# Packed constants and initial states, three filler products, one epsilon moved, and a new step list in a Test-Time-Training layer

## The chip, the cores and the metric

The kernel runs on one core of a Trainium2 chip, as one hand-ordered program for all engines. The metric is the device time of one execution in microseconds (us), taken as the median of three runs. The profile is of one further execution.

## The reference

For each of 4 sequences of 512 tokens and 256 channels the layer computes, in float32:

```
x = x + layernorm(attn(layernorm(x)));   x = x + layernorm(ffn(layernorm(x)))
attn: qkv = x @ Wqkv; q, k = l2norm(silu(.)) per head of 64; v = silu(.)
      lr = softplus(x @ Wlr + c); mom = sigmoid(x @ Wm + bm); scale = silu(x @ Ws + bs)
      for each chunk of 128 tokens, states W0, W1, W2 (64x64 a head), momenta M0, M1, M2:
          out = (silu(q W0^T) * (q W2^T)) W1^T
          dW0, dW1, dW2 = gradients from k, v and lr, plus M * mean(mom);  M = dW
          dW = newton_schulz5(dW):  five times A = X X^T; B = bA + cA A; X = aX + B X
          W  = renorm(W + dW)
      out = rmsnorm(out) * g * scale, plus windowed softmax attention with 128-wide heads
      result @ Wo
ffn:  gelu(x @ proj1^T + b1) @ proj2^T + b2      (1024 hidden)
```

## The kernel before

All five engines walk the same list of steps, `ORDER`. A step is a kind, a chunk and an index (`NA.1.3.0` is kind NA, chunk 1, iteration 3, state 0). Each engine runs the parts of those kinds that it takes a share in and skips the others, so the list fixes the program order on every engine at once; between engines there are only semaphore waits. `bank_plan` derives the PSUM banks from the same list. SyncE (SP) alone doesn't follow the list before the change: its loads and stores stand in a fixed sequence.

The kinds that matter here, with the TensorE (PE) line that a profile shows:

- `LN1`/`LNX` the first layer norm, `XT` its transposes (L536 for chunk 0, L543 later), `QK` (L559) and `VV` (L568) the projections, `TR` (L591) transposes of q, k, v.
- `FW` (L629), `GB` (L604), `DH` (L617), `OUT` (L643), `DW` (L662) the chunk's forward and gradient products; `SS` (L673) the Frobenius norms.
- the Newton-Schulz steps, five iterations over three states in each of chunks 0 to 2: `TX` (L682, four 128x128 transposes), `NA` (L691), `NB` (L701), `NX` (L713). ScalarE (ACT) copies after TX and NX, VectorE (DVE) finishes NA and NB.
- `RN`/`RM` the renorm of the states, `WX` (L723) the transposes of the new states.
- `S`, `PT`, `PV`, `CT`, `WO` (L732, L739, L748, L755, L763) attention and output projection; `NT` (L770), `F1` (L782), `F2`/`F2N` (L793) the feed-forward block and its norm.

`NA`, `NB`, `NX`, `DH`, `FW` and `OUT` run on 64x64 quarters of the PE array, four at a time, `GB` on 64x128 halves, and the others on all 128 rows. `NA`, `NB` and `NX` leave 32 records a step (64x64x64 products), `F1` 4 of 512 columns, `TX` 4.

The start of chunk 0. PE first runs nine 128x128 products of ones (L808), then `XT.0.0`, then `QK.0.0`. SP issues x for sequence 0, all of Wqkv, x for the others, three small weight pieces, seven small constants (b1 in elements of 4 bytes), and, when Wqkv has landed, six pieces of the initial states into `w_in`. DVE's `WI` copies them into `W` in six copies (L1355, L1359), ACT's `WI` squares them (L1022), and `WX.0.0` to `WX.0.2` transpose `W` on PE, with three ACT copies. The first layer norm of a sequence is DVE statistics, then GpSimd (POOL) for variance plus epsilon (L1424) and the power -0.5 (L1419), then DVE.

SP's later sequence is: x again for chunks 0 and 1, x for chunks 2 and 3, the stores of chunk 0, x again for chunk 2, the stores of chunk 1, x again for chunk 3, and the rest of the stores. The loads of `x again` (L451) each wait for the one before to land.

The end, for the last sequence of the last chunk: `F2` on PE, then

```
dve.bn_stats(st4[:, b, :], f2[:, b, :])
dve.bn_aggr(mv4[:, b, :], st4[:, b, :])
pool.tensor_scalar(var[:, sl], mv[:, sl, 1], LN_EPS, None, ALU.add)   # L1424
tt(rstd[:, sl], var[:, sl], neg_half[:, 0:k], ALU.pow)                # L1419
```

then the scaling on DVE and the store.

Of the kernel before, what the change touches and what calls it, by code (L numbers as in the profile page):

```python
# [30 lines left out]
P = 128  # L31
# [3 lines left out]
HD = 64  # L35
# [5 lines left out]
SMALL = 5 * NH  # L41
LN_EPS = 1e-5
# [81 lines left out]
NOT_IN_FIRST = ("x_in", "ln1_stats", "ln1_mv", "ln1_var", "ln1_rstd", "xn", "xT_ps", "xnT", "mm_ps", "mm", "decayed")  # L124
# [4 lines left out]
def steps(text):  # L129
# [7 lines left out]
    LN1.0.0 XT.0.0 LNX.0.0 LN1.0.1 LN1.0.2 CO.0 LN1.0.3 LNX.0.1 QK.0.0 XT.0.1 LNX.0.2 LNX.0.3 VV.0.0 VV.0.1 SI.0.0  # L137
    NQ.0.0 XT.0.2 XT.0.3 QK.0.1 SI.0.1 WI.0 LN1.1 QK.0.2 VV.0.2 NQ.0.1 LNX.1 SI.0.2 NR.0.0 QK.0.3 VV.0.3 NR.0.1 NQ.0.2
    TR.0.0 SM.0 TR.0.1 SI.0.3 MS.0 NQ.0.3 TR.0.2 TR.0.3 XT.1 TR.0.4 TR.0.5 TR.0.6 TR.0.7 NR.0.2 NR.0.3 KL.0.0 KL.0.1
    KL.0.2 KL.0.3 SP.0 WX.0.0 WX.0.1 WX.0.2 S.0.0 S.0.1 VV.1.0 VV.1.1 TR.0.8 TR.0.9 WN.0 FW.0.0 FE.0.0 FE.0.1 DH.0  # L140
    FW.0.1 GB.0.0 GB.0.1 OUT.0.0 OUT.0.1 EL.0.0 EL.0.1 OE.0 QK.1.0 SI.1.0 QK.1.1 EY.0 SI.1.1 S.0.2 ELB.0.0 ELB.0.1
    PT.0.0 PT.0.1 MU.0.0 MU.0.1 MU.0.2 MR.0.0 MR.0.1 MR.0.2 QK.1.2 DW.0.0 DW.0.1 QK.1.3 SS.0.0 S.0.3 SS.0.1 OY.0
    VV.1.2 PV.0.0 PV.0.1 SS.0.2 PT.0.2 PT.0.3 SN.0.0 SN.0.1 VV.1.3 CT.0.0 PV.0.2 PV.0.3 SN.0.2 WO.0.0 TX.0.0.0
    TX.0.0.1 CT.0.1 NA.0.0.0 NA.0.0.1 SI.1.2 CT.0.2 WO.0.1 TX.0.0.2 NB.0.0.0 NB.0.0.1 CT.0.3 NA.0.0.2 NX.0.0.0
    NX.0.0.1 WON.0.0 WON.0.1 L2.0.0 NB.0.0.2 TX.0.1.0 WO.0.2 WO.0.3 NA.0.1.0 L2N.0.0 WON.0.2 WON.0.3 NX.0.0.2 SM.1
    L2.0.1 L2.0.2 TR.1.0 TX.0.1.1 TX.0.1.2 L2.0.3 TR.1.1 NA.0.1.1 NA.0.1.2 NB.0.1.0 L2N.0.1 L2N.0.2 L2N.0.3 TR.1.2
    TR.1.3 NB.0.1.1 NB.0.1.2 NT.0.0 MS.1 NT.0.1 NT.0.2 NT.0.3 NX.0.1.0 NX.0.1.1 NX.0.1.2 TX.0.2.0 NQ.1.0 TX.0.2.1
    TX.0.2.2 NQ.1.1 SI.1.3 F1.0.0 NA.0.2.0 NA.0.2.1 NA.0.2.2 F1.0.1 F1.0.2 LN1.2 NB.0.2.0 NB.0.2.1 NB.0.2.2 NQ.1.2
# [18 lines left out]
    F2.1.3 XT.3 GB.2.0 GB.2.1 EL.2.0 EL.2.1 OUT.2.0 OUT.2.1 S.2.1 ELB.2.0 ELB.2.1 OE.2 QK.3.0 QK.3.1 QK.3.2 MU.2.0
    MU.2.1 MU.2.2 DW.2.0 DW.2.1 PT.2.0 PT.2.1 QK.3.3 MR.2.0 MR.2.1 MR.2.2 SS.2.0 S.2.2 SS.2.1 SS.2.2 S.2.3 OY.2 SN.2.0
    PV.2.0 PV.2.1 SN.2.1 SN.2.2 PT.2.2 VV.3.0 PT.2.3 PV.2.2 CT.2.0 F2N.1.1 CT.2.1 TX.2.0.0 TX.2.0.1 TX.2.0.2 NA.2.0.0
    NA.2.0.1 SI.3.0 NA.2.0.2 WO.2.0 WO.2.1 NB.2.0.0 NB.2.0.1 NB.2.0.2 NX.2.0.0 NX.2.0.1 NX.2.0.2 WON.2.0 WON.2.1  # L170
    L2.2.0 TX.2.1.0 TX.2.1.1 TX.2.1.2 PV.2.3 NA.2.1.0 NA.2.1.1 NA.2.1.2 NQ.3.0 F2N.1.2 L2N.2.0 VV.3.1 VV.3.2 NB.2.1.0
# [1407 lines left out]
```

## Time and profile before

| | before |
|---|---|
| median of three runs | 382.04 us (381.73 to 382.21) |
| span of the profiled execution | 380.1 us |
| what lies around the span, to the median | 1.9 us |
| PE busy | 371.0 us, 98% |
| DVE, ACT, POOL busy | 68%, 56%, 51% |

In the rows below a line is a time, a duration, an engine, a source line and what it writes and reads, with the number of records. In the chain of waits the pieces follow each other in time without overlap, so the length of a piece is the time until the next piece; in the timeline the last product of a group includes its way through the array, so groups overlap by some 0.2 us.

### The profile page before, as it was taken

The page shows a single profiled execution, that of the slowest core. Times are in us where ns is not written, and L with a number is a line of the kernel's source. Part 1 is how long each engine was busy: PE and PEld are TensorE (multiplying, and loading weights), DVE is VectorE, ACT ScalarE, POOL GpSimd, SP SyncE. Part 2 cuts the span into 40 slices and gives each one's busy share as a digit, 9 for nine tenths or more (in the row PEclk, how much of TensorE's full clock was granted, in tenths as well). Part 3 has the DMA queues.
Part 4 walks back from the last instruction along what each step waited for, and adds up shares of the span by engine and source line. Part 5 has one row for each costly group of instructions (what it writes and reads, how often), then busy time and mean ns, then how long its engine had stood idle before and what let it go on. Part 6 is the DMA issues. An engine that isn't in the chain of part 4 may idle for free.

```text
span 380.1 us, 15979 instructions
## 1 busy us (share of the span) xinstructions
PE 371.0 (98%) x6760; PEld 295.4 (78%) x6760; DVE 257.6 (68%) x682; ACT 213.3 (56%) x432; POOL 193.9 (51%) x290
## 2 busy tenths in 40 slices
PE   8999999999999999999999999999999999999994
PEld 5588688856788877878578888688887757988883
DVE  4678998674278699898546746987875492767124
ACT  1799855766512766649743346665358575614500
POOL 4399865356239457475963434364333340557212
PEclk9999999999999999999999999999999999999999
DMA  5562200001000000000000200000000110000101
GB/s 156 121 238 60 83 1 6 3 3 46 16 3 2 3 3 2 3 4 5 16 19 17 71 16 3 2 2 17 20 3 4 40 36 2 0 3 0 57 0 55
DMA packets 12677, 10.84 MB, mean 29 GB/s; under 512 B 4544, under 2 KB 12096, under 8 KB 12608
## 3 DMA queue, kind: packets, MB, share of 16 engines
q1 hardware_dynamic: 12608, 9.83, 8.9%
q8 instruction: 54, 0.88, 1.0%
q14 instruction: 15, 0.12, 0.1%
HBM read 7.73 MB, written 2.10 MB: 26 GB/s over the span
## 4 chain that ended last, share of the span: by engine, by line
PE 86%; DVE 4%; SPq 3%; issue 2%; POOL 2%; ACT 1%; DMA 1%; POOLq 0%; DVEq 0%; ACTq 0%
PE pair L782 15%; PE pair L793 15%; PE pair L713 6%; PE pair L701 6%; PE pair L691 6%; PE pair L559 6%; PE pair L682 5%; PE pair L591 4%; PE pair L763 3%; PE pair L732 3%; PE pair L568 3%; PE pair L748 3%; PE pair L662 2%; PE pair L739 2%; PE pair L629 1%
## 5 line engine op out<-in xcount | busy, mean ns | idle before, releaser
L782 PE MATMUL pair<-xn2T,p1T 128*128 128x512 f32 (+1 forms) x160 | 59.1, 512 | 0.0
L793 PE MATMUL pair<-p2T,h 128*128 128x256 f32 x256 | 57.0, 379 | 0.0
L793 PEld LDWEIGHTS pair<-p2T,h 128*128 128x128 f32 x256 | 48.0, 190 | 6.4 <-issue 0.2
L1424 POOL TENSOR_SCALAR var<-mv 128x1 f32<-128x1 f32 (+1 forms) x55 | 13.1, 239 | 67.1 <-DVE mv L1382 37.4
L1034 ACT ACTIVATE h<-pair,b 128x512 f32<-128x512 f32 (+1 forms) x40 | 23.9, 602 | 36.0 <-PE pair L782 35.9
L782 PEld LDWEIGHTS pair<-xn2T,p1T 128*128 128x128 f32 x160 | 28.7, 190 | 17.1 <-issue 14.8
L1419 POOL TENSOR_TENSOR nq<-ssq,half 128x8 f32<-128x8 f32 (+1 forms) x16 | 24.2, 1513 | 27.5 <-DVE ssq L1141 27.5
L1056 DVE SCALAR_TENSOR_TENSOR A<-pair,eye 128x512 f32<-128x512 f32 x45 | 28.7, 683 | 13.2 <-PE pair L691 13.1
L1419 POOL TENSOR_TENSOR rstd<-var,neg_half 128x1 f32<-128x1 f32 (+1 forms) x55 | 33.5, 609 | 4.6
L1056 DVE SCALAR_TENSOR_TENSOR B<-pair,eye 128x512 f32<-128x512 f32 x45 | 28.9, 684 | 10.2 <-PE pair L701 10.0
L559 PE MATMUL pair<-wqkv,xnT 128*128 128x512 f32 x64 | 31.5, 627 | 0.6 <-ACT xnT L816 0.6
L701 PEld LDWEIGHTS pair<-A 64*64 64x64 f32 x1440 | 23.7, 134 | 7.5 <-issue 4.6
L987 ACT ACTIVATE masked<-masked,nmax 128x256 f32<-128x256 f32 (+1 forms) x32 | 15.1, 474 | 25.5 <-DVE nmax L1298 25.5
L823 ACT ACT_TABLE_LOAD x22 | 28.2, 1283 | 1.1 <-PEq L1569 0.7
L691 PEld LDWEIGHTS pair<-XT 64*64 64x64 f32 x1440 | 23.3, 134 | 6.3 <-issue 5.7
L816 ACT ACTIVATE XT<-pair 128x512 f32<-128x512 f32 x45 | 24.6, 600 | 6.4 <-PE pair L682 6.4
L713 PEld LDWEIGHTS pair<-X,B 64*64 64x64 f32 x1440 | 23.6, 134 | 5.0 <-issue 2.7
L959 ACT ACTIVATE X<-pair 128x512 f32<-128x512 f32 x36 | 19.8, 598 | 13.2 <-PE pair L713 13.1
L701 PE MATMUL pair<-A 64*64 64x64 f32 x1440 | 26.5, 221 | 0.3 <-issue 0.3
L713 PE MATMUL pair<-X,B 64*64 64x64 f32 x1440 | 26.1, 221 | 0.1
L691 PE MATMUL pair<-XT 64*64 64x64 f32 x1440 | 25.8, 221 | 0.3 <-ACT XT L816 0.2
L682 PE MATMUL pair<-ident,X 128*128 128x128 f32 x180 | 24.1, 276 | 0.5 <-ACT X L959 0.3
(165 smaller groups left out, 775.4 us busy)
## 6 DMA issues: line engine op xcount, KB each, us to landing
x_in<-in_L_attn_x_dram SPq DMA_DIRECT2D x16, 128.0 KB, 2.5
x<-in_L_attn_x_dram SPq DMA_DIRECT2D x16, 128.0 KB, 2.1
out_dram<-rows_a SPq DMA_DIRECT2D x16, 128.0 KB, 1.7
p1T<-in_L_ffn_proj_dram SPq DMA_DIRECT2D x1, 1024.0 KB, 4.7
p2T<-in_L_ffn_proj_dram SPq DMA_DIRECT2D x1, 1024.0 KB, 7.4
wqkv<-in_L_attn_Wqkv_dram SPq DMA_DIRECT2D x1, 768.0 KB, 4.8
wo<-in_L_attn_Wo_dram SPq DMA_DIRECT2D x1, 256.0 KB, 7.7
X<-in_L_attn_w_dram SPq DMA_DIRECT2D x6, 32.0 KB, 2.2
```

Source lines behind the costliest of these rows:

```text
L559: mm_ = pe.matmul(ps, xnT[:, k, b * P:(b + 1) * P], wqkv[:, k, 0:512], start=(k == 0), stop=(k == KC - 1))
L682: mm_ = pe.transpose(ps[:, b * P:(b + 1) * P], X[:, g, 2 * b:2 * b + 2, :], ident[:, :])
L691: mm_ = pe.matmul(BANK[bank[0] + row][64 * col:64 * col + 64, n * HD:(n + 1) * HD], xt, xt, start=True, stop=True)
L701: mm_ = pe.matmul(BANK[bank[0] + row][64 * col:64 * col + 64, n * HD:(n + 1) * HD], a, a, start=True, stop=True)
L713: mm_ = pe.matmul(BANK[bank[0] + row][64 * col:64 * col + 64, n * HD:(n + 1) * HD], B[64 * row:64 * row + 64, g, 4 * (row ^ (slot & 1)) + ...
L782: mm_ = pe.matmul(ps[:, at], p1T[:, k, n * P:(n + 1) * P], xn2T[:, k, at], start=(k == 0), stop=(k == KC - 1))
L793: mm_ = pe.matmul(ps[:, 0:DIM], h[:, n, b * P:(b + 1) * P], p2T[:, n, :], start=(n == 0), stop=(n == HC - 1))
L816: return act.activation(dst, src, ACT.Copy)
L823: act.preload_act_table_set(name)
L1034: act.activation(h[:, n, at], BANK[bank[0]][:, at], ACT.Gelu, bias=b1[:, n:n + 1]).then_inc(S["h"].sem, 1)
L1056: return dve.scalar_tensor_tensor(out=out_, in0=in0, scalar=scalar, in1=in1, op0=op0, op1=op1)
L1419: return pool.tensor_tensor(out_, in0, in1, op)
```

## The change

- **Loads.** The host lays out three arrays: `Wall` (Wqkv, Wlr, Wm, Ws side by side), `packed` (all constants as each lane holds them, 356 values a lane), and `states` (the initial W, as the kernel holds it for all sequences, and its transposes, 3072 values a lane). SP issues x of sequence 0, the 512 columns of q and k, x of the others, the 276 other columns, `packed`, W, and the transposes in two pieces, and no longer waits for Wqkv in between. Bytes that these loads move: 128, 512, 3 times 128, 276, 178, 768, 512 and 256 KB.
- **Work gone.** DVE's `WI` (six copies), one memset, `WX.0.0` to `WX.0.2` (12 PE transposes, three ACT copies). ACT's `WI` waits for the load of W.
- **Three products on ones.** After the transposes of `XT.0.0` PE runs three products of 128x128 on 64 columns into bank 7.
- **Last epsilon.** For the last sequence of the last chunk DVE adds epsilon, POOL only takes the power.
- **SP follows the list.** `XA` (x again), `XI` (x for a chunk) and the stores (`F2N`) are steps of the list. `XA` of chunk 2 or 3 waits for all four `outb` of two chunks before.
- **A new list.** The same steps otherwise, in another order; `EY` and `WN` move to the front, `KL.0.3` behind `EL.0.1`, and the Newton-Schulz steps of a state are no longer taken three by three.

```
-            sp.dma_start(wqkv[:, :, 0:3 * DIM], Wqkv...).then_inc(ld_qkv, 16)
+            sp.dma_start(wqkv[:, :, 0:512], Wall[:, 0:512]...).then_inc(ld_qkv, 16)
...
+            sp.dma_start(wqkv[:, :, 512:], Wall[:, 512:]...).then_inc(ld_v, 16)
+            sp.dma_start(packed_in[:, :], packed).then_inc(ld_misc, 16)
+            sp.dma_start(W[:, :, :, :], states[:, 0:1536]...).then_inc(ld_w, 16)
+            sp.dma_start(WT02[:, :, :, :, :], states[:, 1536:2560]...).then_inc(ld_wT, 16)
+            sp.dma_start(W1T[:, :, :, :], states[:, 2560:3072]...).then_inc(ld_wT, 16)
+            XI(1)
...
+            def XA(c):
+                if c >= 2:
+                    sp.wait_ge(*S["outb"](c - 2, BATCH))
+                for b in range(BATCH):
+                    if b or c:
+                        sp.wait_ge(*S["x_again"](c, 16 * b))
+                    sp.dma_start(x1[:, c % 2, b, :], ...).then_inc(S["x_again"].sem, 16)
...
                     mm_.then_inc(S["first_xT"].sem, 1)
+                    if b == 0:
+                        for n in range(3):
+                            pe.matmul(BANK[7][:, 0:64], ones[:, :], ones[:, 0:64], start=True, stop=True)
...
             def WI(c):
-                act.wait_ge(*S["W"](0, 3))
+                act.wait_ge(ld_w, 16)
...
             def F2(bank, c, b):            # DVE
+                if ends(c, b):
+                    dve.wait_ge(*S["f2_mv"](c, b + 1))
+                    dve.tensor_scalar(var4[:, b:b + 1], mv4[:, b, 1:2], LN_EPS, None, ALU.add)...
...
             def F2(c, b):                  # POOL
+                if ends(c, b):
+                    wait_apart(pool, S["f2_var"](c, b + 1))
+                    tt(rstd4[:, b:b + 1], var4[:, b:b + 1], neg_half[:, 0:1], ALU.pow)...
+                    return
```

The start of the list, and a stretch in chunk 1's Newton-Schulz steps:

```
-    LN1.0.0 XT.0.0 LNX.0.0 LN1.0.1 LN1.0.2 CO.0 LN1.0.3 LNX.0.1 QK.0.0 XT.0.1 LNX.0.2 LNX.0.3 VV.0.0 VV.0.1 SI.0.0
+    LN1.0.0 XA.0 XT.0.0 WI.0 LNX.0.0 QK.0.0 XT.0.1 CO.0 LN1.0.1 LN1.0.2 XT.0.2 LNX.0.1 SI.0.0 LN1.0.3 EY.0
+    LNX.0.2 LNX.0.3 WN.0 VV.0.0 NQ.0.0 XT.0.3 QK.0.1 VV.0.1 LN1.1 VV.0.2 SI.0.1 NQ.0.1 QK.0.2 SI.0.2 NR.0.0
...
-    NX.1.3.2 TX.1.4.0 TX.1.4.1 TR.2.4 TX.1.4.2 TR.2.5 TR.2.6 MP.2 KL.2.3 F2N.0.2 NA.1.4.0 NA.1.4.1 NA.1.4.2 TR.2.7
-    F1.1.6 NB.1.4.0 F2N.0.3 NB.1.4.1 NB.1.4.2 TR.2.8 F1.1.7 NX.1.4.0 NX.1.4.1 NX.1.4.2 RN.1.0 RN.1.1 RM.1.0 RN.1.2
+    TX.1.4.0 F1.1.5 NR.2.3 TX.1.4.1 F2N.0.3 NB.1.3.2 NA.1.4.0 MM.2 NA.1.4.1 NX.1.3.2 NB.1.4.0 KL.2.2 F1.1.6
+    TX.1.4.2 F1.1.7 NA.1.4.2 NB.1.4.1 TR.2.4 MP.2 NX.1.4.0 NB.1.4.2 RN.1.0 NX.1.4.1 F2.1.0 TR.2.5 RN.1.1 TR.2.6
```

In the new list `XA.2` stands in chunk 0's third Newton-Schulz iteration, ahead of all `F2N.0` steps. `F2N.0.3` stands 15 PE steps ahead of `F2.1.0`, whose DVE part waits until chunk 0's stores have landed.

## Rows read from the trace of the kernel before

**Rows 1.** The page: the span, and TensorE's share of it.

```profile
span 380.1 us, 15979 instructions
PE 371.0 (98%) x6760; PEld 295.4 (78%) x6760; DVE 257.6 (68%) x682; ACT 213.3 (56%) x432; POOL 193.9 (51%) x290
```

**Rows 2.** Windows, TensorE alone: busy time and, behind it, the granted clock.

```profile
54.00:120.00 66.00, 65.59 (x1653) 1.00 0.04 11
```

**Rows 3.** Timeline of TensorE, 0 to 30 us; in brackets the idle time before.

```profile
1.04 4.21 PE L808 MATMUL pair<-ones 128*128 128x128 f32 x18 [1.04 <-DVE ones L1054]
5.28 0.66 PE L536 MATMUL pair<-ident,rows_b 128*128 128x128 f32 x2
6.50 3.75 PE L559 MATMUL pair<-wqkv,xnT 128*128 128x512 f32 x4 [0.56 <-ACT xnT L816]
...
17.16 1.88 PE L559 MATMUL pair<-wqkv,xnT 128*128 128x512 f32 x4
```

**Rows 4.** Timeline of ScalarE, 0 to 50 us.

```profile
5.98 0.38 ACT L816 ACTIVATE xnT<-pair 128x256 f32<-128x256 f32 x1 [3.98 <-PE pair L536]
10.29 0.60 ACT L816 ACTIVATE raw<-pair 128x512 f32<-128x512 f32 x1 [3.94 <-PE pair L559]
...
16.24 1.01 ACT L1022 ACTIVATE B<-W 128x256 f32<-128x256 f32 x3
```

**Rows 5.** Chain of waits, chunk 0's second Newton-Schulz iteration.

```profile
77.36 1.56 PE pair L691 x96
78.92 3.63 PE pair L782 x8
82.55 1.56 PE pair L701 x96
84.11 3.63 PE pair L782 x8
87.74 1.56 PE pair L713 x96
89.30 1.48 PE pair L682 x12
90.78 1.72 PE pair L782 x4
92.50 1.56 PE pair L691 x96
```

**Rows 6.** Chain of waits, chunk 2's fourth and fifth iterations.

```profile
276.38 0.87 PE pair L682 x8
...
289.27 1.09 PE pair L701 x64
...
290.83 1.91 PE pair L782 x4
292.74 0.62 PE pair L701 x32
```

**Rows 7.** Chain of waits, the transposes of the initial states.

```profile
25.33 1.31 PE pair L723 x12
```

**Rows 8.** Timeline of SyncE's queue: loads of x again, stores.

```profile
181.41 28.27 SPq L491 DMA_DIRECT2D out_dram<-rows_a  x4
209.72 7.29 SPq L451 DMA_DIRECT2D x<-in_L_attn_x_dram  x4
```

**Rows 9.** Windows, TensorE alone, while the feed-forward weights land; last GB/s.

```profile
21.00:22.00 1.00, 1.00 (x11) 1.00 1.08 386
```

**Rows 10.** Chain of waits, from the last product's end.

```profile
361.14 13.83 PE pair L793 x64
374.97 0.02 issue
375.00 0.44 DVE rows_a L1378
...
376.33 0.22 POOL var L1424
376.55 0.04 issue
376.59 0.83 POOLq L236
```

More of the change, by code:

```diff
@@ L167 @@
[L167 to L171, printed above, removed]
@@ new lines @@
+    FE.1.1 QK.2.1 ELB.1.0 ELB.1.1 OUT.1.0 OE.1 MU.1.0 OUT.1.1 MU.1.1 DW.1.0 MU.1.2 MR.1.0 DW.1.1 PT.1.0 S.1.2
+    MR.1.1 QK.2.2 PT.1.1 S.1.3 SS.1.0 MR.1.2 QK.2.3 OY.1 SS.1.1 PV.1.0 SN.1.0 SS.1.2 PT.1.2 PV.1.1 CT.1.0 VV.2.0
+    TX.1.0.0 SN.1.1 VV.2.1 NA.1.0.0 CT.1.1 SN.1.2 TX.1.0.1 WO.1.0 SI.2.0 NB.1.0.0 NA.1.0.1 TX.1.0.2 F2N.0.0
+    PT.1.3 PV.1.2 NA.1.0.2 WON.1.0 NB.1.0.1 WO.1.1 PV.1.3 NX.1.0.0 NB.1.0.2 NX.1.0.1 CT.1.2 WON.1.1 L2.1.0
+    NQ.2.0 TX.1.1.0 SI.2.1 CT.1.3 VV.2.2 TX.1.1.1 SI.2.2 NA.1.1.0 WO.1.2 NA.1.1.1 NB.1.1.0 WON.1.2 NX.1.0.2
@@ new lines @@
+    RN.2.1 RM.2.0 RN.2.2 RM.2.1 RM.2.2 TR.3.5 F1.2.4 F1.2.5 WX.3.0 FE.3.0 F1.2.6 WX.3.1 WX.3.2 F1.2.7 FE.3.1
+    FW.3.0 FW.3.1 PT.3.0 PT.3.1 MS.3 OE.3 S.3.2 OUT.3.0 OUT.3.1 S.3.3 F2.2.0 F2.2.1 OY.3 PV.3.0 PT.3.2 F2.2.2
+    PV.3.1 PT.3.3 CT.3.0 F2N.2.0 PV.3.2 F2N.2.1 CT.3.1 WO.3.0 WO.3.1 WON.3.0 PV.3.3 WON.3.1 L2.3.0 CT.3.2 L2.3.1
+    L2N.3.0 L2N.3.1 F2.2.3 CT.3.3 NT.3.0 WO.3.2 NT.3.1 WO.3.3 WON.3.2 F1.3.0.0 F1.3.1.0 F1.3.2.0 F1.3.3.0
+    WON.3.3 F1.3.4.0 L2.3.2 F1.3.5.0 L2.3.3 F1.3.6.0 NT.3.2 L2N.3.2 NT.3.3 F1.3.7.0 F1.3.0.1 F1.3.1.1 F1.3.2.1
@@ L184 @@
+    L2N.3.3 F1.3.3.1 F2N.2.2 F2N.2.3 F1.3.4.1 F2.3.0 F1.3.5.1 F1.3.6.1 F1.3.7.1 F2N.3.0 F2.3.1 F2.3.2 F2N.3.1
+    F2N.3.2 F2.3.3 F2N.3.3
 """)
@@ L231, with layer_kernel @@
 PLAN = bank_plan(ORDER)
-def layer_kernel(nc, x, Wqkv, Wlr, Wm, bm, Ws, bs, Wo, w0, w1, w2, o_norm_g, qk_scale, qk_offset,
-                 proj1T, proj1_bias, proj2T, proj2_bias, out):
+def layer_kernel(nc, x, Wall, packed, states, Wo, proj1T, proj2T, out):
     with ExitStack() as ctx:
@@ L434, in mask_of, with ends @@
             return mask[:, seen(c):2 * P] if slot(c) else mask[:, P:3 * P]
+        def ends(c, b):
+            return c == CHUNKS - 1 and b == BATCH - 1
         def learns(c):
@@ L459, in rows_in, with F2N @@
                     sp.dma_start(x_in[:, b, :], x[b, bass.ts(c, CHUNK), :]).then_inc(S["x_in"].sem, 16)
+            def F2N(c, b):
+                sp.wait_ge(*S["outb"](c, b + 1))
+                sp.dma_start(out[b, bass.ts(c, CHUNK), :], outb[:, b, :]).then_inc(S["stored"].sem, 16)
+            parts = {"XI": XI, "XA": XA, "F2N": F2N}
             sp.dma_start(x_in[:, 0, :], x[0, 0:CHUNK, :]).then_inc(first_x[0], 16)
-            sp.dma_start(wqkv[:, :, 0:3 * DIM], Wqkv.rearrange("(k p) n -> p k n", p=P)).then_inc(ld_qkv, 16)
+            sp.dma_start(wqkv[:, :, 0:512], Wall[:, 0:512].rearrange("(k p) n -> p k n", p=P)).then_inc(ld_qkv, 16)
@@ L485, in _, with run @@
             sp.dma_start(wo[:, :, :], Wo.rearrange("(k p) n -> p k n", p=P)).then_inc(ld_wo, 16)
-            rows_again(0)
-            def stores(c):
-                for b in range(BATCH):
-                    sp.wait_ge(*S["outb"](c, b + 1))
-                    sp.dma_start(out[b, bass.ts(c, CHUNK), :], outb[:, b, :]).then_inc(S["stored"].sem, 16)
-            rows_again(1)
-            rows_in(2)
-            rows_in(3)
-            stores(0)
-            rows_again(2)
-            stores(1)
-            rows_again(3)
-            stores(2)
-            stores(3)
+            def run(order):
+                for kind, c, *arg in order:
+                    if kind in parts:
+                        parts[kind](c, *arg)
+            run(ORDER)
             sp.wait_ge(*S["stored"](CHUNKS, 0))
```

172 lines of the change are left out of this document (81 added, 91 removed).

## The prediction

 So PE's order of work is the critical path, and other engines count only where they make PE wait. PE's idle time is 9.1 us: 1.04 before the first product and 0.56 before the first QK [rows 3], 5.1 from the last product's end at 374.97 to the end [rows 10], and 2.4 spread over everything else. The reader is to see that there is little idle time to win, and that what PE spends on a piece of work is what counts.
>
> Busy does not mean at peak, though. I walked through PE's steps from XT.0.0 at 5.28 to 374.97, which is 369.7 us, and gave each step the shortest time that a step of its kind with such neighbours has anywhere in this trace. That adds up to 357 us, so 12 us are waits or slow stretches: 1.8 in QK.0.0, 1.0 just before it, and about 9 in small pieces, most of them under 0.5 us. These 9 us are an estimate, and all that a better order can give back.
>
> **The work that goes.** The transposes of the initial states are 12 records, 1.31 us of PE in the chain [rows 7]: **-1.3**. DVE's copies and ACT's copies go too; both engines are far from full [rows 1], so that alone is worth nothing.
>
> **What the new list costs on PE.** This is the term that decides. In the chain a block of 64x64 products takes 0.62 us for one step, 1.09 for two, 1.56 for three [rows 5, 6]: 0.47 a step, and 0.15 once a block. Blocks on all 128 rows pay too when they stand between such blocks: F1 with 4 records takes 1.72 where it ends a run begun by TX, 1.91 alone between 64-row blocks, and two of them 3.63, not 3.44; TX with 12 records takes 1.48, where 8 take 0.87, so 12 would take 1.31 [rows 5, 6]. So each 128-row run pays 0.15 to 0.19, and each time PE goes over to 64-row products and back costs 0.30 to 0.34 us. The stretch from 77.36 to 92.50 checks it: 15.14 us, of which 9 Newton-Schulz steps at 0.47, five F1 at 1.72 and 1.31 of transposes are 14.14; three returns cost the other 1.0 [rows 5].
>
> I counted in both lists how many separate runs of 64-row steps (NA, NB, NX, DH, GB, FW, OUT) PE meets: 52 before, 70 after. The new list mixes states and iterations singly with transposes and other work, where the old one took three at a time. 18 more at 0.32: **+5.8** (5.4 to 6.1). No cover hides it, since PE itself is the bound.
>
> The Trainium skill, page TensorEngine Tiling (Array Packing), section Key Properties, says that changing the tiling mode drains TensorE; by its wording every change of mode counts, also those to DW's 128x64 tiles and GB's 64x128, of which I count 114 before and 147 after. It gives no price; with half of the 0.32 for each of 33 more the term would be +5.3, not +5.8. It speaks against this change as the rows do.
>
> **The start.** Nine products on ones take 4.21 us as 18 records, and QK.0.0 3.75 us, where a later QK takes 1.88; the transposes of XT.0.0 are slow as well [rows 3]. That is the 1.2 GHz level, though the windows show no lower granted clock there. PE was at work from 1.04 on, with one gap of 0.56 us before QK.0.0. Three products of 64 columns fit in that gap: at this rate some 0.1 a record, six records, 0.6 us. PE's wait is for ACT's copy, which ends at 6.36 [rows 4], so they delay nothing. If the full rate comes by 7, QK.0.0 gains up to 1.8 us; if it comes as late as before, nothing. The trace has no such case, so these are the bounds.
>
> Not all of it can be kept. ACT's WI now stands ahead of the copies of QK.0.0 and XT.0.1, and waits for W. Up to W's end the queue moves 2.2 MB (the sizes in the section on the change); at the 386 GB/s of [rows 9] this is 5.8 us, from about 2 or 3 us on, so W lands at 8 to 9. The squares take 1.0 [rows 4], then the copy of q and k 0.6 and of xnT 0.4 must follow before QK.0.1: about 11. PE at full rate is done with QK.0.0, two XT, VV.0.0 and XT.0.3 at about 10, and stands still for 1 us. At the old rate ACT is free at 6.36 to 10.29 [rows 4], which covers WI, and nothing is lost or won. I take half: **-0.9** (0 to -1.8).
>
> The Trainium skill, page TensorE: Matmul & The Clock Gate, Part 1, says that throttled is the default state and sustained activity releases it, whatever the number of products. By that rule the filled gap would bring the full rate earlier, and the term could be the whole -1.8.
>
> **Other waits.** EY and WN leave POOL's busy stretch for its idle beginning, the initial states need no preparation, and Newton-Schulz steps of different states follow each other in a pipeline. I compared, for every producer and consumer on PE, how much PE work lies between them in both lists: in both nearly all distances are about the shortest that the trace shows to suffice (1.0 us for NA to NB and NB to NX). So the new list is no worse, and may avoid some of the 9 us. Half of these pieces are under 0.1 us and stay in any order. I take **-2.0**, with bounds of -5 (all but these gone) and +1.5.
>
> **SP's queue.** XA.2 stands ahead of chunk 0's stores and waits for all four outb. When F2N.0.3 is done, four loads must go first, 7.3 us for three of the intervals and so some 9.5 with the last [rows 8], then four stores at about 0.5, and a landing of 2: some 12 us after outb. F2.1.0's part on DVE needs them, 15 PE steps and its own 3.5 us later, by my prices 13.6 us after F2N.0.3. outb itself costs 1 to 2 us. It just fits: 0, and if it does not, DVE stands still, and with it the renorm of chunk 1. The transposed states have landed long before FW.0.0, the first to read them, which follows all of chunk 0's projections.
>
> **The end.** After the last product come DVE, POOL's epsilon (0.22 us, with 0.15 before it), POOL's power and DVE [rows 10]. On DVE the epsilon saves one step to another engine but takes its own time: **-0.1** (0 to -0.2). The subtraction behind it still ends ahead of POOL's power of 0.83.
>
> **Sum.** -1.3 + 5.8 - 0.9 - 2.0 - 0.1 = +1.5 on a span of 380.1: 381.6. Around the span lie 1.9 us to the median of the runs, 382.04. So 383.5.
>
> **Rivals.** First, the other side: the new order takes nearly all waits away, and the full rate comes early. -1.3 + 5.8 - 1.8 - 5.0 - 0.1 = -2.4: 379.6. For it speaks the finer pipeline and POOL's lighter middle; against it, that PE has only 2.4 us of true idle time there [rows 1]. It decides from the point where start and waits together give back more than 5.2 us. Chance 0.25. Second, the three products release nothing and the order saves no waits: -1.3 + 5.8 - 0.1 = +4.4: 386.4. For it: 4.2 us of products and XT did not release the clock before [rows 3]. Chance 0.12. Third, the stores of chunk 0 land too late: if the loads take 2.4 us each and outb comes 2 us after F2N.0.3, DVE waits 1 to 2 us at F2.1.0: 385.0. Chance 0.08. The forecast has 0.55.
>
> **Numbers.** 0.2% is 0.76 us, about what a measurement of this kernel can tell from no change. The forecast's own spread is 381 to 385.5; of its 0.55 some 0.15 lies within 0.76 us of 382.04 and 0.03 below. With the first rival that makes faster 0.28, within 0.2% 0.16, slower 0.56. The range runs from 380.0 to 386.0: it leaves out about half of the first and second rivals.
>
> **What would show it.** In the changed profile the Newton-Schulz lines L691, L701, L713 should appear in the chain as many blocks of 32 and 64 records at 0.62 and 1.09, and F1 or transposes between them with 0.15 to 0.19 extra; PE busy should be about as long as now or longer, though 12 transposes are gone. QK.0.0 should take 1.9 to 3.75 us and be followed by a wait for ACT behind the squares. The chunk 0 stores come after four loads, and DVE should not wait for them. The prediction is wrong if the extra returns are cheaper than 0.3 us where both sides are single steps, or if the waits that remain are under 4 us in all.

## The result, and the profile after

The changed kernel takes 386.77 us (median of four, 385.51 to 387.03), the kernel before beside it 382.12: ratio 1.0112, with a 95% interval of 1.0095 to 1.0129. So slower, as forecast, but by 4.7 us and not by 1.5, and above the range's 386.0.

The page of the changed kernel, to be read against [rows 1]:

```profile
span 385.1 us, 15941 instructions
...
PE 375.3 (97%) x6754; PEld 296.7 (77%) x6754; DVE 259.2 (67%) x676; ACT 213.6 (55%) x429; POOL 194.3 (50%) x289
...
PEclk9899999999999999999999999999999999999999
...
q8 instruction: 54, 0.88, 1.0%
```

PE is busy 4.3 us longer with six records fewer, and still 3.1 us longer in a second profile in which the clock does not fall: the order costs more than the transposes gave back. The second of its 40 slices, 9.6 to 19.3 us, has a lower granted clock, which no slice of before has. Why is in the timeline of TensorE:

```profile
6.85 1.94 PE L553 MATMUL pair<-wqkv,xnT 128*128 128x512 f32 x4
...
12.69 2.92 PE L553 MATMUL pair<-wqkv,xnT 128*128 128x512 f32 x4 [2.23 <-ACT xnT L810]
```

and in that of ScalarE:

```profile
10.76 1.03 ACT L1017 ACTIVATE B<-W 128x256 f32<-128x256 f32 x3 [4.35 <-DMA W<-in_states_dram]
11.70 0.57 ACT L810 ACTIVATE raw<-pair 128x512 f32<-128x512 f32 x1
12.18 0.65 ACT L810 ACTIVATE xnT<-pair 128x256 f32<-128x256 f32 x2
```

QK.0.0 runs in 1.94 us (3.75 in [rows 3]). Meanwhile ACT stands 4.35 us for W, which lands at 10.7, and the copies for QK.0.1 come behind the squares. W was issued at 4.14 us; the page has the 6.6 us to its landing:

```profile
W<-in_states_dram SPq DMA_DIRECT2D x1, 768.0 KB, 6.6
```

```profile
13.50:17.00 3.50, 3.50 (x7) 1.90 (x6) 0.69 (x1) 2.26 (x5) 2.92 (x2) 0.51 0.31 79
```

The middle looks as the forecast said. The chain of waits in chunk 0's third iteration, against [rows 5]:

```profile
85.03 1.72 PE pair L776 x4
86.75 0.62 PE pair L695 x32
87.38 0.47 PE pair L685 x32
87.84 1.91 PE pair L776 x4
89.76 0.44 PE pair L676 x4
90.19 0.44 PE pair L585 x4
90.63 0.62 PE pair L695 x32
```

Blocks of one or two 64-row steps stand where three stood; the first costs 0.62, one behind it 0.47, and F1 alone between them 1.91. But further on the chain has a thing that the forecast didn't know:

```profile
303.46 0.62 PE pair L707 x32
304.09 0.23 PE pair L695 x16
304.32 0.67 issue
304.99 0.40 PE pair L695 x10
```

PE stops for 0.67 us in the middle of one NB step, where no instruction waits for a semaphore.

SP's queue did as forecast: four loads of 6.5 us, then the stores of chunk 0, all issued by 214.5, three us ahead of DVE's part of F2.1.0, which waits for PE and for no transfer:

```profile
204.84 6.54 SPq L456 DMA_DIRECT2D x<-in_L_attn_x_dram  x4
211.42 3.07 SPq L468 DMA_DIRECT2D out_dram<-rows_a  x4
...
217.50 0.42 DVE L1359 TENSOR_TENSOR rows_a<-pair,packed_in 128x256 f32<-128x256 f32 x1 [1.77 <-PE pair L787]
```

The tail's chain has DVE's epsilon, 0.16 us for POOL's 0.22 and its 0.15 ahead of it [rows 10]. POOL's power behind it takes 0.59 us in the chain, where it took 0.83 behind POOL's own epsilon. From the last product to the end are 4.8 us instead of 5.2:

```profile
381.48 0.16 DVE var L1366
```

**The account.** I walked through all PE steps of the changed kernel as the prediction did for before, each at the cheapest price that its kind and neighbours have in the trace of before. The first three rows are this count and no view of the profile; it ends PE's work 0.1 to 0.2 us ahead of the chain's last product, which the fifth row takes up. A second profile of the same program (e11 below) is beside it. A fetch is the load of a stretch of PE's own instructions; the experiments on the stops show why it stands here.

| us | before | changed | changed, again |
|---|---|---|---|
| PE's steps at the cheapest price | 357.4 | 362.4 | 362.4 |
| above it, up to TX.0.0.0 | 5.3 | 7.5 | 5.6 |
| above it, behind TX.0.0.0 | 6.8 | 4.8 | 6.2 |
| of these, stops of over 0.15 inside 64x64 blocks at a fetch | 0.5 | 1.9 | 3.1 |
| ahead of the first transpose, and the tail | 10.6 | 10.4 | 10.4 |
| span | 380.1 | 385.1 | 384.6 |

### The profile page after: what moved, and what is told of

Its sections match the earlier page's. It is cut to its first block, busy times and chain, and to the rows that moved or that the text cites. A ratio compares the mean times of both kernels' runs of the same rounds, so it can differ in the third digit from the quotient of the medians.

```text
span 385.1 us, 15941 instructions
## 1 busy us (share of the span) xinstructions
PE 375.3 (97%) x6754; PEld 296.7 (77%) x6754; DVE 259.2 (67%) x676; ACT 213.6 (55%) x429; POOL 194.3 (50%) x289
## 4 chain that ended last, share of the span: by engine, by line
PE 95%; ACT 0%; DVE 0%; issue 0%; POOLq 0%; DVEq 0%; ACTq 0%
PE pair L776 15%; PE pair L787 15%; PE pair L553 7%; PE pair L695 7%; PE pair L685 6%; PE pair L707 6%; PE pair L676 6%; PE pair L585 5%; PE pair L562 4%; PE pair L757 4%; PE pair L726 3%; PE pair L742 3%; PE pair L656 2%; PE pair L623 2%; PE pair L733 2%; PE pair L598 2%
## 5 line engine op out<-in xcount | busy, mean ns | idle before, releaser
L1051 DVE SCALAR_TENSOR_TENSOR B<-pair,eye 128x512 f32<-128x512 f32 x45 | 30.5, 684 | 18.3 <-PE pair L695 18.0
L1029 ACT ACTIVATE h<-pair,packed_in 128x512 f32<-128x512 f32 (+1 forms) x40 | 24.1, 602 | 33.1 <-PE pair L776 32.9
L1051 DVE SCALAR_TENSOR_TENSOR A<-pair,eye 128x512 f32<-128x512 f32 x45 | 30.5, 687 | 14.9 <-PE pair L685 14.5
L810 ACT ACTIVATE XT<-pair 128x512 f32<-128x512 f32 x45 | 26.5, 594 | 15.4 <-PE pair L676 15.2
L685 PE MATMUL pair<-XT 64*64 64x64 f32 x1440 | 30.1, 221 | 0.3 <-issue 0.3
L695 PE MATMUL pair<-A 64*64 64x64 f32 x1440 | 29.8, 222 | 0.7 <-issue 0.7
L685 PEld LDWEIGHTS pair<-XT 64*64 64x64 f32 x1440 | 25.3, 134 | 6.1 <-issue 5.7
L707 PE MATMUL pair<-X,B 64*64 64x64 f32 x1440 | 29.4, 221 | 0.0
L676 PE MATMUL pair<-ident,X 128*128 128x128 f32 x180 | 27.3, 276 | 0.0
L676 PEld LDWEIGHTS pair<-ident,X 128*128 128x128 f32 x180 | 21.0, 141 | 6.6 <-issue 4.5
```

Source lines behind the costliest of these rows:

```text
L676: mm_ = pe.transpose(ps[:, b * P:(b + 1) * P], X[:, g, 2 * b:2 * b + 2, :], ident[:, :])
L685: mm_ = pe.matmul(BANK[bank[0] + row][64 * col:64 * col + 64, n * HD:(n + 1) * HD], xt, xt, start=True, stop=True)
L695: mm_ = pe.matmul(BANK[bank[0] + row][64 * col:64 * col + 64, n * HD:(n + 1) * HD], a, a, start=True, stop=True)
L707: mm_ = pe.matmul(BANK[bank[0] + row][64 * col:64 * col + 64, n * HD:(n + 1) * HD], B[64 * row:64 * row + 64, g, 4 * (row ^ (slot & 1)) + ...
L810: return act.activation(dst, src, ACT.Copy)
L1029: act.activation(h[:, n, at], BANK[bank[0]][:, at], ACT.Gelu, bias=b1[:, n:n + 1]).then_inc(S["h"].sem, 1)
```

## The experiments

Ratios are to the kernel before, on the same chip. The interval stands in brackets.

### Which part of the change it is

**e2_old_list**: the changed kernel with the list of before, `WX.0.*` left out, `XA` and `XI` where SP had them, and the last two steps as in the new list:

```diff
 ORDER = steps("""
-    LN1.0.0 XA.0 XT.0.0 WI.0 LNX.0.0 QK.0.0 XT.0.1 CO.0 ...
+    XA.0 XA.1 XI.2 XI.3 LN1.0.0 XT.0.0 LNX.0.0 LN1.0.1 LN1.0.2 CO.0 ...
```

> The changed kernel with the list of before (without WX.0.0 to WX.0.2; XA.0, XA.1, XI.2, XI.3 first, XA.2 and XA.3 behind F2N.0.3 and F2N.1.3; the last two steps as in the new list). WI.0 stands late in it. Theory A (each return from 128-row to 64-row products costs PE 0.3 us or more, 18 more of them in the new list, and the waits that the new list saves are 2 us): 378 to 379.5 us. Theory B (the new list costs nothing in itself; loads and start do it): 382 to 385 us.

Measured: 379.72 us, 0.9928 [0.9910, 0.9946]. It is the fastest kernel here, 0.7% ahead of before, and 0.2 us above the range that I expected. Its page:

```profile
span 378.2 us, 15942 instructions
```

So the change is two. Everything but the list (the loads, the transposes gone, the epsilon and the three products) is worth -2.8 us together (379.72 less 382.50 beside it), and the new list costs +7.0 (386.77 less 379.72).

**e3_before_filler**: the kernel before with the three products on ones.

```diff
                     mm_.then_inc(S["first_xT"].sem, 1)
+                    if b == 0:
+                        for n in range(3):
+                            pe.matmul(BANK[7][:, 0:64], ones[:, :], ones[:, 0:64], start=True, stop=True)
```

> The kernel before with the three products on ones added behind XT.0.0 and nothing else. Theory A (they close the gap in which the clock was not yet released): QK.0.0 takes under 2.5 us instead of 3.75, the full rate stays, 380.3 to 381 us. Theory B (the early stage is not bound by PE, the gain is given back before the first Newton-Schulz step): QK.0.0 is fast and the time is 382 us. Theory C (they release nothing): 382 us with QK.0.0 at 3.75.

Measured: 382.32, 0.9995 [0.9986, 1.0004]. Nothing, though QK.0.0 took 1.98 us in its profile: TX.0.0.0 begins at 54.0 us there and at 53.9 in the profile of before. With the old list the early full rate buys nothing, as theory B has it.

**e14_old_list_no_filler**: e2 without these products (the reverse of the diff above).

> The changed kernel's loads with the old list and without the three products, against 379.7 with them. If the products do nothing for the clock, and the old list is little sensitive to where fetches fall, 379.7 within 0.7. If they release the clock earlier, QK.0.0 takes 3.7 us again and the time is 380.5 to 381.5.

Measured: 380.85, 0.9962 [0.9949, 0.9975], 1.1 us above e2. It is not the clock: QK.0.0 ran at full rate all the same, and was slow in a kernel that has the products (e13). The timelines of the two:

```profile
6.35 1.96 PE L551 MATMUL pair<-wqkv,xnT 128*128 128x512 f32 x4 [0.56 <-ACT xnT L808]
```

```profile
6.97 3.64 PE L554 MATMUL pair<-wqkv,xnT 128*128 128x512 f32 x4
```

What e14 has and e2 not is one stop of 0.86 us inside an NX block at 58.1. That was a first sign of what follows.

### The price of a return

**e5_returns_block** and **e6_returns_spread**: the kernel before with eight more steps of 32 products on 64x64 tiles in chunk 3, whose results nobody reads, in a row behind F1.3.0.1, or one behind each F1.3.n.1.

```diff
+            def DM(bank, c, i):
+                for n in range(4):
+                    for row, col in QUADS:
+                        xt = XT[64 * row:64 * row + 64, 0, 2 * n + (row ^ col), :]
+                        pe.matmul(BANK[bank[0] + row][64 * col:64 * col + 64, n * HD:(n + 1) * HD], xt, xt, ...)
```

> The kernel before with eight more steps of 32 products 64x64 (as NA, on XT, into free banks, read by nobody) in chunk 3, all eight in a row behind F1.3.0.1. A block of n such steps should cost 0.47 n + 0.15 and the run behind it 0.1 to 0.19: 4.0 to 4.1 us more, 386.1 us. If the returns cost nothing: 3.7 us more.

> The same eight steps, one behind each of F1.3.0.1 to F1.3.7.1, so that there are eight returns instead of one. Theory A (0.30 to 0.35 us a return): 2.1 to 2.5 us more than with the eight in a row, 388.4 us. Theory B (returns cost little; the new list lost its time in waits): the same as in a row, within 0.5 us.

Measured: 388.12, 1.0145 [1.0128, 1.0162], and 388.54, 1.0158 [1.0143, 1.0173]. The chain of e6:

```profile
354.84 0.62 PE pair L730 x32
355.47 1.06 PE pair L797 x4
356.53 0.62 PE pair L730 x32
357.15 1.06 PE pair L797 x4
```

A half F1 of 0.86 takes 1.06, the block 0.62 for 0.47: 0.36 us a return by the chain, a little over the 0.32 of the forecast. By the time it is less: 6.1 us over before, less eight steps at 0.47, leave 2.3, or 0.29 a return. e6 came out as expected, e5 2.0 us over. The two kernels differ by only 0.4, because the row of eight pays in another coin; the chain of e5:

```profile
356.07 2.13 PE pair L730 x133
358.19 0.54 issue
358.74 2.08 PE pair L730 x123
360.81 1.06 PE pair L797 x4
361.88 0.47 issue
```

### The start

**e1_wi_later**: in the changed kernel WI.0 behind SI.0.1, and WN.0 behind NR.0.0.

```diff
-    LN1.0.0 XA.0 XT.0.0 WI.0 LNX.0.0 QK.0.0 ...
+    LN1.0.0 XA.0 XT.0.0 LNX.0.0 QK.0.0 ... SI.0.1 WI.0 ... NR.0.0 WN.0 ...
```

> The changed kernel with two steps of its list moved: WI.0 (ACT squares W once it has landed) behind SI.0.1, WN.0 behind NR.0.0. Theory A (the start was lost because ACT stood behind WI until W landed at 10.7 us, so that PE stood still from 10.3 to 12.7 and then ran at 1.2 GHz from 13.5 to 17.0): PE goes on at 10.5, the granted clock stays 1.00 from 6.7 on, PE's start loses some 3.5 to 4 us less, 382.5 to 383.3 us. Theory B (the start is late for another reason, the loads or the layer norm): the wait of PE before QK.0.1 stays over 1.5 us, 386 to 387 us.

Measured: 389.61, 1.0193 [1.0159, 1.0227]: slower still. The wait ahead of QK.0.1 is gone, but the power of WN.0 (2.3 us on POOL) now stands ahead of what TR.0.7 needs, and the same pair of events comes 14 us later, a stand and a lower clock (timeline, then windows; a stand is idle time of PE ahead of a step):

```profile
27.10 0.63 PE L586 MATMUL pair<-ident,silu 128*128 128x128 f32 x4 [2.21 <-POOL silu L1404]
```

```profile
27.50:31.00 3.50, 3.50 (x73) 3.22 (x71) 2.04 (x6) 2.55 (x6) 3.41 (x5) 0.52 0.30 93
```

That is the smaller part. At TX.0.0.0 its profile is 1.2 us behind the changed kernel's first, at the end 5.1 us. PE has the same steps in the same order in both, but the stops inside 64x64 blocks (below) add up to 5.6 us here and 1.9 there. The profile is also of the slowest of its six executions, which lie between 387.7 and 392.0.

**e9_squares_later_pow_later** and **e13_squares_power_in_slack**: the power gets a step of its own, WP.0, behind NX.0.1.0 (e9) or ahead of LN1.2 (e13).

```diff
-            parts = {..., "KL": KL, "WN": WN, "EL": EL, ...}
+            parts = {..., "KL": KL, "WP": WN, "EL": EL, ...}
```

> The changed kernel with ACT's squares of W behind SI.0.1 and DVE's sum of them behind NR.0.0, as in the earlier try, but POOL's power of 12 columns now stands behind NX.0.1.0, in POOL's slack, and not ahead of the norms of chunk 0. My theory: the wait of 2.2 us ahead of QK.0.1 goes, no wait of 2.4 us for POOL follows at 24, the granted clock doesn't fall to 0.50 before 50 us, and the kernel runs 2 to 3.5 us faster than the changed kernel: 383.3 to 384.8. Rival: the time stays at 386 to 389, because the new list loses as much to the fetch of instructions as in the run without the three products; then the profile shows over 3 us of issue in the middle of 64x64 blocks.

> The kernel with ACT's squares and DVE's sum later, and POOL's power now ahead of LN1.2, where POOL stands idle for 5 us (in the last try it stood in POOL's busy stretch again and cost 0.74 us ahead of NB.0.1.1). My theory: no wait on PE for ACT or POOL's power is left; 0.5 to 1 us less than in the last try, 385.4 to 386.0, more if the idle of 1.4 us in NA.0.2.0 falls elsewhere. Rival: the fetch moves onto another block and the time stays at 386.4 or rises.

Measured: 386.41, 1.0096 [1.0083, 1.0110], and 385.38, 1.0074 [1.0061, 1.0086]. e9 missed its range of 383.3 to 384.8, and its rival held; e13 is at the lower edge of its own and keeps 1.4 us of its repair. Of e9's 3.3 us less up to TX.0.0.0 (4.2 over the cheapest price, 7.5 in the first profile of the changed kernel; against the second it is 1.4 less) only 0.4 arrived. Much of it went into stops, 3.5 us in all, the largest in its chain:

```profile
71.64 0.46 PE pair L686 x14
72.10 1.20 issue
73.30 0.51 PE pair L686 x15
```

**e7_newstart_oldrest** and **e8_oldstart_newrest**: the loads of the change, one list up to TX.0.0.0 and the remaining steps in the order of the other.

```python
steps = start[:start.index("TX.0.0.0")]
steps += [s for s in rest if s not in steps]
```

> The changed kernel's loads, its list up to the first transpose of the Newton-Schulz iteration (TX.0.0.0), and behind that the steps in the order of the old list. My theory: the changed kernel loses in two separate places, about 2 to 3 us in the start (ACT's squares ahead of the copies for QK.0.1) and the rest behind TX.0.0.0 (15 more returns to 64x64 products, 4.9 us, less 2 to 3 us of waits saved). This kernel keeps the bad start and three early returns (1.0 us) and should run at 382.5 to 383.5, some 3 us above the old list on the new loads (379.7). Rival: the start costs nothing that lasts, because a later wait takes it back; then 380.0 to 381.0. Second rival: only the whole new list is slow, by where the instruction transfers fall; then no number follows, and the idle marked as issue in the middle of blocks of 64x64 products differs by over 1 us from both parents.

> The changed kernel's loads, the old list up to the first transpose of the Newton-Schulz iteration (TX.0.0.0), and behind that the steps in the order of the new list. My theory: 386.8 less the start (2 to 3 us) and less three returns (1.0): 382.8 to 383.8. Rival, that the new list's later steps cost nothing by themselves: 380 to 381. Rival, that the start costs nothing: 385.8.

Measured: e7 382.31, 0.9992 [0.9978, 1.0006]; e8 386.94, 1.0123 [1.0103, 1.0143]. e7 came out 0.2 us below its range: the new start costs 2.6 us over e2, by the account 1.1 in three returns and 1.7 in waits, the one for ACT above all; the clock did not fall here:

```profile
12.98 1.96 PE L554 MATMUL pair<-wqkv,xnT 128*128 128x512 f32 x4 [2.51 <-ACT xnT L811]
```

e8 came out 3.1 us above its range. Its start is 3.2 us better than in the changed kernel's first profile, but between TX.0.0.0 and the end of chunk 0's iterations it has 4.8 us over the cheapest price where the changed kernel has 1.2 or 2.3. Of these 1.4 are stops inside blocks. The rest are waits, since PE arrives earlier and DVE, POOL and ACT do not. So the two halves of the list do not add: over e2 the new start costs 2.6 us, the new rest 7.2, and both together 7.0. The timeline of e8:

```profile
53.30 0.70 PE L686 MATMUL pair<-XT 64*64 64x64 f32 x32 [0.78 <-ACT XT L811]
...
55.37 0.69 PE L696 MATMUL pair<-A 64*64 64x64 f32 x32 [0.79 <-DVE A L1052]
...
63.63 0.58 PE L686 MATMUL pair<-XT 64*64 64x64 f32 x24 [1.06 <-ACT XT L811]
```

### The stops inside blocks

**e4_new_no_filler** and **e12_waits_for_filler**: the changed kernel without the three products, and with 12 waits on a long raised semaphore in their place.

```diff
-                        for n in range(3):
-                            pe.matmul(BANK[7][:, 0:64], ones[:, :], ones[:, 0:64], start=True, stop=True)
+                        for n in range(12):
+                            pe.wait_ge(warm, 1)
```

> The changed kernel without the three products on ones. Theory A (with ACT held behind WI, the early rate only lengthens PE's stand before QK.0.1 to 2.4 us, after which the rate falls again): QK.0.0 takes 3.75, the stand is about 1 us, the rate doesn't fall, and the time is 1 to 2 us shorter than with them, 385 us. Theory B (the products are a gain in any case): 388 us or more.

> The changed kernel with 12 satisfied waits in the place of the three products on ones, so that the stream has as many instructions and no products. If the run without the products was slower (389.0) because all later instructions moved up by 12, this one has the changed kernel's gaps again and runs at 386.3 to 387.3. If the products themselves matter, it runs at 388.5 to 389.5 like the one without them. The waits may be laid down as fewer than 12 instructions; then the gaps stand at neither's blocks.

**e10_waits64**: the changed kernel with 64 such waits ahead of QK.0.1.

> The changed kernel with 64 more waits on PE ahead of QK.0.1, on a semaphore that has long been raised: they move nothing but the place of all later instructions in PE's stream, and lie inside the 2.2 us for which PE stands there anyway. If where the instruction transfers fall matters, the idle in the middle of 64x64 blocks moves to other blocks, and the sum of it changes by 1 to 3 us, and the time with it: 385.8 to 389. If it doesn't matter, the time is the changed kernel's within 0.5 us (386.8) and the same blocks show the same idle.

**e11_changed_again**: the changed kernel, unchanged.

> The changed kernel itself, once more. If the place of the fetches in the instruction stream decides, the idle of over 0.2 us in the middle of 64x64 blocks stands at the same blocks as in the first profile (at some 69.6, 74.2, 287 and 304 us) with about the same lengths, 1.9 us in sum, and the time is 386.8 within 0.5. If it is chance from run to run, other blocks show it.

Measured: e4 389.02, 1.0169 [1.0148, 1.0190]; e12 389.05, 1.0167 [1.0146, 1.0188]; e10 391.28, 1.0233 [1.0207, 1.0259]; e11 386.77, 1.0110 [1.0095, 1.0126]. e4 is slow as its theory B has it, with 4.7 us of stops in its blocks where the changed kernel's first profile has 1.9. In e11's profile PE stood 1.70 us ahead of QK.0.1, the clock did not fall, and PE was at TX.0.0.0 1.9 us earlier than in the first profile. It kept 0.5 of it. The stop at 304 came again at the same products (chain):

```profile
303.59 0.23 PE pair L695 x16
303.82 0.67 issue
304.49 0.40 PE pair L695 x10
```

So the places belong to the program and not to chance; the sum does not, 3.1 us here and 1.9 before, since some of the other stops have other lengths. And e10 says that they follow the place of instructions in the stream: 64 waits (laid down as 32 instructions) between the same steps add 3.8 us of span, 0.9 of it where they stand. (Its time is 2.3 us above the range that I expected.) e12 did not separate what it was meant to: its 12 waits are 6 instructions, so its stream is neither that of the changed kernel (13,925 instructions) nor that of e4 (13,913).

Then I counted. The records of PE, the products, weight loads and waits, are all there but, as I take it, 8 at the start, which no view shows; without them each place below is 8 lower. From the start of the stream, counted from 0, each stop of over 0.32 us inside a block of 64x64 products and ahead of no semaphore wait, in all 20 profiles, stands ahead of instruction 201 or 202 of a group of 256, and each such stop ends 2.2 to 3.0 us after a transfer of the instruction queue began. That queue moves 54 packets, 0.88 MB, so 16,384 bytes each, for 13,925 instructions: 64 bytes an instruction, 256 a transfer. In none of the 20 profiles do two of these transfers begin less than 3.3 us apart; the shortest distance is 3.30 to 3.67 us, by profile. A 64-row step is 64 instructions in 0.47 us; 256 would take 1.9 us, less than that distance. Groups of nothing else occur in no list, since other steps stand between, but dense stretches come near it, and it is in these that PE stops. The Trainium skill, page Advanced Engine Details and Errata, section ISA Cache, gives lines of 16 KB, 256 instructions; the places and the packets agree with it.

From the timeline of a trace, with these stops taken out, I then computed what other shifts of the stream would cost, if PE can't go from one such place to the next in under 3.4 to 3.6 us. By that count, an estimate, the kernel before stands in the only good stretch, some 50 of 256 places wide, where it pays nothing; further off it would pay up to 10 us.

**e15_before_shift120**, **e16_before_shift228**, **e17_before_shift60**, **e18_changed_shift140**: the order of all steps is kept; only the nine long products on ones at the very start, whose results nobody reads, are in part replaced by small ones. Here e15 (5 and 34; e16: 1 and 65; e17: 5 and 19; e18: 5 and 39):

```diff
-            for n in range(9):
+            for n in range(5):
                 pe.matmul(BANK[7][:, (n % 4) * P:(n % 4 + 1) * P], ones[:, :], ones[:, :], start=True, stop=True)
+            for n in range(34):
+                row, col = QUADS[n % 4]
+                pe.matmul(BANK[6 + row][64 * col:64 * col + 64, 64 * (n // 4 % 8):64 * (n // 4 % 8) + 64],
+                          ones[64 * row:64 * row + 64, 0:64], ones[64 * row:64 * row + 64, 0:64], start=True, stop=True)
```

> The kernel before, its list unchanged, with four of the nine products on ones at the start replaced by 34 small ones on 64x64 tiles (as long in time, 120 instructions more). Theory: instructions come in groups of 256, and PE can't get from one group's end to the next in under some 3.4 to 3.6 us. On the trace of before, with all later instructions 120 places further on, that adds 8 to 10 us of idle: 390 to 392.5, with idle in the middle of blocks at some 10 places (near 61, 101, 200, 268, 302 us over 0.9 each). Rival: the place in the stream doesn't matter, 382.4 within 0.7.

> The kernel before with eight of the nine products on ones replaced by 65 small ones, 228 instructions more, which is 28 places short of a full group of 256. By the same count on the trace of before this adds no idle: 382.4 within 0.7 (up to 1 us more if the small products take longer than the eight). Rival, that any 120 or 228 more instructions, or small products in the place of long ones at the start, cost time by themselves: as slow as the shift by 120 or slower.

> The kernel before with four of the nine products replaced by 19 small ones, 60 instructions more. By the same count 5.8 to 7.4 us of idle: 388 to 390. Rival: 382.4 within 0.7.

> The changed kernel with four of the nine products replaced by 39 small ones, 140 instructions more. By the same count 4.9 to 6.2 us more idle than it has now: 391.5 to 393. Rival: 386.8 within 0.7.

Measured: e15 394.39, 1.0312 [1.0295, 1.0329]; e16 383.74, 1.0037 [1.0023, 1.0050]; e17 388.38, 1.0159 [1.0139, 1.0179]; e18 391.73, 1.0240 [1.0218, 1.0261]. Three pay: e17 and e18 what the count said, e15 1.9 us above its range. The control, e16, pays 1.4 us and has no more stops than before: up to TX.0.0.0 its profile is 1.9 us worse, since PE stood 2.17 us ahead of TR.0.0, and the clock was at 0.5 from 21.4 to 24.8 us. Two places of e15's chain, in a stretch where before has no stop of over 0.2 us:

```profile
290.76 0.41 PE pair L713 x15
291.17 1.06 issue
292.23 0.50 PE pair L713 x17
...
295.50 0.55 PE pair L691 x29
296.05 1.28 issue
297.33 0.33 PE pair L691 x3
```

And its page, then that of e16, which has more products and less busy time:

```profile
span 391.6 us, 16099 instructions
...
PE 374.3 (96%) x6820; PEld 297.1 (76%) x6820; DVE 258.2 (66%) x682; ACT 213.8 (55%) x432; POOL 194.0 (50%) x290
```

```profile
span 381.8 us, 16207 instructions
...
PE 370.3 (97%) x6874; PEld 295.8 (77%) x6874; DVE 257.5 (67%) x682; ACT 213.3 (56%) x432; POOL 194.7 (51%) x290
```

The stops are of one profile each, the times the medians:

| kernel | instructions moved | stops inside blocks, us | time, us |
|---|---|---|---|
| before | 0 | 0.5 | 382.3 |
| e16 | +228 | 0.5 | 383.7 |
| e17 | +60 | 6.1 | 388.4 |
| e15 | +120 | 8.7 | 394.4 |
| changed, e11 | 0 | 1.9, 3.1 | 386.8 |
| e12 | -6 | 5.7 | 389.1 |
| e4 | -12 | 4.7 | 389.0 |
| e10 | +32 | 5.7 | 391.3 |
| e18 | +140 | 6.4 | 391.7 |
| e1 | 0 | 5.6 | 389.6 |
| e9 | 0 | 3.5 | 386.4 |
| e13 | 0 | 2.9 | 385.4 |
| e2 | old list, 0 | 0.9 | 379.7 |
| e14 | old list, -12 | 1.5 | 380.9 |

e1, e9 and e13 have the changed kernel's stream of PE, and their stops stand at the same places; only the lengths differ, with when PE arrives and from one execution to the next.

At the worst of the three shifts that were run the kernel before is 2.7 us slower than the changed kernel at its own (394.4 and 391.7). Its lead at shift 0 is in part where its stream happens to lie.

## Why the prediction was right in direction and wrong in size

- **The work that goes**, -1.3: right by the count: e2's steps at the cheapest price are 1.3 below those of before. No run has it alone.
- **The returns**, +5.8: the direction rests on this term, and it held. By the account the new list costs 6.3 at the cheapest prices, 0.5 more; e6 measured 0.36 a return by its chain and 0.29 by its time, which would be 6.5 or 5.2 for 18.
- **The start**, -0.9 (0 to -1.8): this is the first step that failed. Its chain of reasoning was right, ACT's squares ahead of the copies and PE's wait behind an early QK.0.0, but W landed at 10.7 and 10.5 us where I had put 8 to 9, so the wait was 1.7 to 2.2 us and not 1. I had let the loads land one after the other, 2.2 MB up to W's end. That much had indeed moved by 9.0 us, but part of it belonged to other loads: of W's 16 parts the first landed at 8.8 and the last at 10.7, and the first piece of the transposes, issued 0.5 us behind W, was in at 10.8. At W's landing 2.9 MB had moved, at 336 GB/s from 2.0 us on and not at 386. The three products were not free either: in the first profile, at the old rate, they took 1.23 us and QK.0.0 began 0.44 us behind ACT's copy, where it was 0.14 in before and in the second profile. The wait took back more than the clock gave: the term is +2.2 in the first profile, where the clock fell again, and +0.3 in the second. It should have had a bound above nothing. On the side of the gain e3 shows nothing for an early full rate with the old list. e7 gives +1.7 for the start without returns.
- **Other waits**, -2.0: the first profile has -2.0 and the second -0.6. That the first agrees is luck, since it is a sum of two that I didn't separate: by the account other waits fell by 3.4 and 3.2, as the finer pipeline promised, and the stops at instruction fetches rose by 1.4 and 2.6. The 9 us of "small pieces" held few of these stops, because before has few; the changed kernel could only gain more of them. This is the second step that failed, a term of 1.4 to 2.6 us that was missing. Such stops took back most of the repairs of the start in e9, all in e4, and in e8 together with waits for the other engines; e13 kept 1.4 us.
- **SP's queue**, 0: right. **The end**, -0.1 (0 to -0.2): more, -0.36. Of it 0.12 is the epsilon, and 0.24 is POOL's power, which I had not thought to be shorter. XT.0.0 begins 0.06 later, so -0.3 stands in the sum.
- Two readings of mine were off and change nothing: from 374.97 to the end are 5.2 us and not 5.1, and 369.7 less 357 leaves 12.7 us of waits and slow stretches and not 12.
- **Sum**: -1.3 + 6.3 + 2.2 - 2.0 - 0.3 is +4.9 for the first profile's +5.0 of span, and with +0.3 and -0.6 it is +4.4 for the second's +4.5.
- **The rivals.** The second ("the three products release nothing and the order saves no waits", 386.4) had the nearest time, for the wrong reasons: QK.0.0 did run fast and waits were saved. The first failed by its own condition, that start and waits give back over 5.2 us. The third did not happen.

Left open: why e15 pays 2 us more than counted, why two transfers begin no less than 3.3 us apart, and how far ahead of its use one is asked for. The time between two of these places was mostly 3.3 us or more, but a few stretches of 2.2 to 3.1 us had no stop. The 6.3 us of the new list's prices are a count on traces, borne out by the price in e6; no run has the new order with fewer returns. How much of the 7.0 us of the new list would remain at the best place for each list was not run; by the count, an estimate, both already stand near their best.

## What to carry to other kernels

Where one engine runs many short instructions, its instruction stream is a resource with a rate (here its transfers of 256 instructions began at least 3.3 us apart): count where the dense stretches lie against the places of its fetches, and after an edit of a few instructions at the start look for idle marked as issue inside blocks before blaming the order of work. Test an order and what comes with it apart: here everything but the order was worth -2.8 us and the order cost 7.0. A step put ahead of a copy on an in-order engine is as early as its slowest input, so price it by when that transfer lands, with the loads issued just behind it counted in, with a bound on either side of nothing.

## What the hardware showed that I had not expected

- Two loads of 768 and 512 KB, issued 0.5 us apart by one engine, landed 0.1 us apart in one profile (10.7 and 10.8 us) and 0.5 in the other (10.5 and 11.0); 512 KB alone would take 1.5 us at the 336 GB/s of that stretch.
